# Heads of width 16: operands of 49 rows in two halves of the partitions

## What is computed

```
xr = rope(x)                                   # over the 256 features, before the projection
q, k, v = (xr @ W.T + b for (W, b) in (q, k, v))      # 4 x 16 heads x 512 x 16
p = softmax(q @ k.T / 4)                       # 512 x 512 per head
y = layernorm(x + (p @ v) @ Wo.T + bo)
```

## Time and profile before

| | us |
|---|---|
| three timed runs | 1989.82, 1995.94, 1994.33 (median 1994.33) |
| profiled execution, its own time | 2008.87 |
| its span, first to last instruction | 2007.5 |
| PE busy in the span | 1674.5 (83%) |
| DVE, ACT, POOL busy | 1149.6, 1011.2, 983.3 |

### The profile page before, as it was taken

One profiled execution on the slowest core, in us unless ns is written; L12 is line 12 of the kernel. 1 busy time (PEld: TensorE's weight loads), 2 busy tenths in 40 slices (PEclk: granted clock), 3 DMA queues, 4 the chain that ended last, 5 costly groups with the idle time before them and its releaser, 6 DMA issues. The chain is left out here.

```text
span 2007.5 us, 23647 instructions
## 1 busy us (share of the span) xinstructions
PE 1674.5 (83%) x7418; PEld 1222.8 (61%) x7419; DVE 1149.6 (57%) x2237; ACT 1011.2 (50%) x1933; POOL 983.3 (49%) x832
## 2 busy tenths in 40 slices
PE   5698896699972798989996999989999997589992
PEld 2476675587761465656764666656656665566661
DVE  4665655566645676767745665665575573542223
ACT  2154442455521376766774776666676673142222
POOL 1200000344324266676882775675585584058885
PEclk9899998799996599999998999999999998679996
DMA  2300100544424332222102110121020120248777
GB/s 82 128 12 0 32 22 21 186 109 114 121 45 124 81 82 65 72 64 74 43 21 87 28 44 22 33 62 25 25 67 25 25 60 22 62 98 193 183 181 172
DMA packets 96785, 146.15 MB, mean 73 GB/s; under 512 B 22711, under 2 KB 61820, under 8 KB 93830
## 3 DMA queue, kind: packets, MB, share of 16 engines
q1 hardware_dynamic: 66448, 104.92, 18.1%
q0 software_dynamic: 18432, 26.36, 7.5%
q10 hardware_dynamic: 11782, 13.37, 2.2%
HBM read 101.83 MB, written 36.41 MB: 69 GB/s over the span
## 5 line engine op out<-in xcount | busy, mean ns | idle before, releaser
L2261 POOL TENSOR_TENSOR STp_lo_use<-ST_use,STp_hi_use 128x512 fp32r<-128x512 f32 x256 | 337.7, 1328 | 202.2 <-ACT ST_use L2091 200.9
L1737 POOL TENSOR_TENSOR STp_lo<-ST,STp_hi 128x512 fp32r<-128x512 f32 x192 | 248.2, 1313 | 106.1 <-ACT ST L1512 104.7
L2156 DVE TENSOR_REDUCE nmax_use<-bank 128x1 f32<-128x512 f32 x256 | 173.4, 679 | 111.7 <-PE bank L1996 107.2
L2087 ACT ACTIVATE STp_hi_use<-bank 128x512 fp32r<-128x512 f32 x256 | 152.9, 597 | 163.1 <-PE bank L2022 159.3
L1630 DVE TENSOR_REDUCE nmax<-bank 128x1 f32<-128x512 f32 x256 | 170.9, 683 | 53.8 <-PE bank L1426 53.1
L1426 PE MATMUL bank<-rows_k,rows_q 65*128 65x512 f32 x256 | 135.9, 539 | 38.3 <-DVE nmax L1630 20.5
L2091 ACT ACTIVATE ST_use<-bank 128x512 f32<-128x512 f32 x256 | 151.8, 593 | 2.0 <-POOL STp_lo_use L2261 2.0
L1509 ACT ACTIVATE STp_hi<-bank 128x512 fp32r<-128x512 f32 x192 | 117.0, 609 | 58.0 <-PE bank L1437 57.6
L924 POOL TENSOR_SCALAR veps<-mv 128x4 f32<-128x4 f32 x4 | 0.9, 228 | 253.1 <-DVE mv L873 253.1
L1996 PE MATMUL bank<-ks,qs 128*128 128x512 f32 x256 | 110.5, 432 | 10.2 <-DMA ks<-ks 9.6
L1512 ACT ACTIVATE ST<-bank 128x512 f32<-128x512 f32 x192 | 118.2, 616 | 0.0
(11 more groups left out here) (443 smaller groups left out, 4644.5 us busy)
## 6 DMA issues: line engine op xcount, KB each, us to landing
stage<-in_W SPq DMA_DIRECT2D x16, 1024.0 KB, 4.9
Wgu<-in_Wgu SPq DMA_DIRECT2D x32, 384.0 KB, 3.4
rows_q<-hop_scratch SPq DMA_DIRECT2D x32, 256.0 KB, 4.3
ks<-ks SPq DMA_DIRECT2D x64, 128.0 KB, 2.3
rinv<-rinv_scratch SPq DMA_DIRECT2D x64, 128.0 KB, 2.9
rows_k<-hop_scratch SPq DMA_DIRECT2D x24, 256.0 KB, 5.3
hop_scratch<-qkp_hi SPq DMA_DIRECT2D x20, 256.0 KB
Wda<-in_Wdn SPq DMA_DIRECT2D x32, 128.0 KB, 3.8
```

Of the source, the lines that this page charges most:

```text
L1737: G.tensor_tensor(parts_of(u)[1], ST[u % TB], plain(parts_of(u)[0]), ALU.subtract).then_inc(low.sem, low.inc(u))
L2087: A.activation(STp[u % NHI][0], bk.ap, ACT.Exp)
L2156: V.tensor_reduce(nmax[:, (h % 2) * TB + j:(h % 2) * TB + j + 1], bk.ap, AX.X, ALU.max, negate=True).then_inc(bk.free, 1)
L2261: G.tensor_tensor(STp[u % NHI][1], ST[u % NFULL], plain(STp[u % NHI][0]), ALU.subtract).then_inc(low["pool"].sem, low["pool"].inc(u))
```

## The change

Three blocks of 16 rows take the place of four: q high, q low, q high against k high, k high, k low. The product of the two low parts is left out, and so is the row of zeros, so that the maxima are products over 48 rows and the scores over 49. The two tiles have 128 partitions and half as many slots: heads 0, 1 of each quarter lie in partitions 0 to 48, heads 2, 3 in partitions 64 to 112. `ST_LAG` grows by one step to 24, so the scores are six heads behind the maxima, and the two products of one step use different halves. The projections of the next batch move one step later. A hop of k is two copies as for q; a quarter's operands come in four DMAs each for q and k (128 or 64 KB), and the row of maxima in two. POOL sets all of `rows_k` to one at the start of the stage, in place of the two memsets. The tiles are allocated in another order.

```diff
-    PARTS, MAX_ROW, ROWS = 4 * HD, 4 * HD + 1, 4 * HD + 2
+    PARTS, MAX_ROW, ROWS, HALF = 3 * HD, 3 * HD, 3 * HD + 1, P // 2
-    ST_LAG = SPAN + 7
+    ST_LAG = SPAN + 8
...
-        rows_q, rows_k = sb("rows_q", [ROWS, H1, S], f32r), sb("rows_k", [ROWS, H1, S], f32r)
+        rows_q, rows_k = sb("rows_q", [P, H1 // 2, S], f32r), sb("rows_k", [P, H1 // 2, S], f32r)
...
-        HOPS = {0: ((0, 0), (1, 1)), 1: ((0, 0), (1, 1), (0, 2))}
+        HOPS = ((0, 0), (1, 1))
...
+        def rows_of(rows, h, count):
+
+            first = h // HG % 2 * HALF
+            return rows[first:first + count, h // HS * HG + h % HG, :]
...
-        STACK = ((28, (0, 0), (0, 0)), (31, (1, 0), (0, 1)), (34, (0, 1), (1, 0)), (37, (1, 1), (1, 1)))
+        STACK = ((29, (0, 0), (0, 0)), (32, (1, 0), (0, 1)), (35, (0, 1), (1, 0)), (38, (1, 1), (1, 1)))
...
-                    PE.matmul(bk.ap, rows_q[0:MAX_ROW, h, j * P:(j + 1) * P], rows_k[0:MAX_ROW, h, :], start=True, stop=True).then_inc(bk.full, 1)
+                    PE.matmul(bk.ap, rows_of(rows_q, h, PARTS)[:, j * P:(j + 1) * P], rows_of(rows_k, h, PARTS), start=True, stop=True).then_inc(bk.full, 1)
...
-                    PE.matmul(bk.ap, rows_k[:, h, kt * P:(kt + 1) * P], rows_q[:, h, :], start=True, stop=True).then_inc(bk.full, 1)
+                    PE.matmul(bk.ap, rows_of(rows_k, h, ROWS)[:, kt * P:(kt + 1) * P], rows_of(rows_q, h, ROWS), start=True, stop=True).then_inc(bk.full, 1)
...
+                        A.wait_ge(zeroed.sem, zeroed["rows"])
                         stack_rows(A, 0, i, 1)
...
-            hs = slice(i * HS, (i + 1) * HS)
-            for k in range(2):
-                first = k * n * HD
-                engine.dma_start(plain((rows_q, rows_k)[n][2 * k * HD:2 * (k + 1) * HD, hs]), hop_d[b % 2, n, hs, first:first + 2 * HD].rearrange("h f s -> f h s")).then_inc(stacked[i].sem, stacked[i].step)
+            for p in range(2):
+                hs, at = slice(i * HS + p * HG, i * HS + (p + 1) * HG), slice(i * HG, (i + 1) * HG)
+                for first, count in ((0, 2), (2, 1)) if n == 0 else ((0, 1), (1, 2)):
+                    to = p * HALF + first * HD
+                    engine.dma_start(plain((rows_q, rows_k)[n][to:to + count * HD, at]), hop_d[b % 2, n, hs, 0:count * HD].rearrange("h f s -> f h s")).then_inc(stacked[i].sem, stacked[i].step)
...
         def pool():
+            G.memset(plain(rows_k), 1.0).then_inc(zeroed.sem, zeroed.inc("rows"))
+            G.wait_ge(zeroed.sem, zeroed["rows"])
...
-                    G.memset(plain(rows_q[PARTS:ROWS]), 0.0).then_inc(g_own.sem, g_own.inc("s4 rows_q"))
-                    G.memset(plain(rows_k[PARTS:ROWS]), 1.0).then_inc(zeroed.sem, zeroed.inc("rows"))
-                    G.wait_ge(zeroed.sem, zeroed["rows"])
...
-                        SP.dma_start(plain(rows_q[MAX_ROW:MAX_ROW + 1, i * HS:(i + 1) * HS, :]).rearrange("p h (j q) -> p (h j) q", q=P), plain(rowbuf[i % 2])).then_inc(rowed[i % 2].sem, rowed[i % 2].inc((b, i)))
+                        for p in range(2):
+                            row = p * HALF + MAX_ROW
+                            SP.dma_start(plain(rows_q[row:row + 1, i * HG:(i + 1) * HG, :]).rearrange("p h (j q) -> p (h j) q", q=P), plain(rowbuf[i % 2][p * HG * TB:(p + 1) * HG * TB])).then_inc(rowed[i % 2].sem, rowed[i % 2].inc((b, i, p)))
```

More of the change, by code:

```diff
@@ L1257, in pair @@
             return kit.pair(name, shape, ph)
-        rows_q, rows_k = sb("rows_q", [ROWS, H1, S], f32r), sb("rows_k", [ROWS, H1, S], f32r)
+        rows_q, rows_k = sb("rows_q", [P, H1 // 2, S], f32r), sb("rows_k", [P, H1 // 2, S], f32r)
+        names = ("Wq1", "Wk1", "Wv1")
+        scale = {"Wq1": HD ** -0.5}
+        W = {n: pair(n, [P, DC, D]) for n in names}
+        cs, xT, part, srcp = sb("cs", [P, 2, S]), sb("xT", [P, DC, S]), sb("part", [P, DC, S]), pair("srcp", [P, DC, S])
         Vone = sb("Vone", [P, TB, H1, P], f32r)
@@ L1267, in self_heads @@
         rowbuf = [sb("rowbuf%d" % z, [SPAN, P], f32r) for z in range(2)]
-        names = ("Wq1", "Wk1", "Wv1")
-        scale = {"Wq1": HD ** -0.5}
-        W = {n: pair(n, [P, DC, D]) for n in names}
         bo, bv = sb("bo", [P, D]), sb("bv", [P, D])
         bqkv, bq = sb("bqkv", [P, 3, DC]), sb("bq", [P, DC])
-        cs, xT, part = sb("cs", [P, 2, S]), sb("xT", [P, DC, S]), sb("part", [P, DC, S])
         attT = turned
         stage = [turned[:, :, 0:D], part[:, :, 0:D]]
-        srcp, qkp = pair("srcp", [P, DC, S]), pair("qkp", [P, DC, S])
+        qkp = pair("qkp", [P, DC, S])
         Vc = sb("Vc", [P, TB, D])
@@ L1293, in self_heads @@
         low = Signal(kit, "s4_low", [u for u in range(END) if not whole[u]])
-        rowed = [Signal(kit, "rowed%d" % z, [(b, i) for b in range(B) for i in range(z, QUARTERS, 2)], step=16) for z in range(2)]
+        rowed = [Signal(kit, "rowed%d" % z, [(b, i, p) for b in range(B) for i in range(z, QUARTERS, 2) for p in range(2)], step=16) for z in range(2)]
         weighed = Signal(kit, "s4_weighed")
@@ L1300, in self_heads @@
         stack_high = Signal(kit, "stack_high", [(b, n, g) for b in range(B) for n, g in (((0, 0), (1, 0), (0, 1), (1, 1)) if b == 0 else ((0, 0), (0, 1), (1, 0), (1, 1)))])
-        HOPS = {0: ((0, 0), (1, 1)), 1: ((0, 0), (1, 1), (0, 2))}
-        hopped = [[Signal(kit, "hopped%d_%d" % (n, g), [(b, k) for b in range(B) for k in range(len(HOPS[n]))], step=16) for g in range(DC)] for n in range(2)]
-        stacked = [Signal(kit, "stacked%d" % i, [(b, n) for b in range(B) for n in range(4)], step=16) for i in range(QUARTERS)]
+        HOPS = ((0, 0), (1, 1))
+        hopped = [[Signal(kit, "hopped%d_%d" % (n, g), [(b, k) for b in range(B) for k in range(len(HOPS))], step=16) for g in range(DC)] for n in range(2)]
+        stacked = [Signal(kit, "stacked%d" % i, [(b, n) for b in range(B) for n in range(8)], step=16) for i in range(QUARTERS)]
         placed = Signal(kit, "placed", [(b, g) for b in range(B) for g in range(GROUPS)])
@@ L1422, in pe @@
                     if j == 0 and h % HS == 0:
-                        PE.wait_ge(stacked[h // HS].sem, stacked[h // HS][b, 3])
+                        PE.wait_ge(stacked[h // HS].sem, stacked[h // HS][b, 7])
                     if n:
                         PE.wait_ge(bk.free, n)
-                    PE.matmul(bk.ap, rows_q[0:MAX_ROW, h, j * P:(j + 1) * P], rows_k[0:MAX_ROW, h, :], start=True, stop=True).then_inc(bk.full, 1)
+                    PE.matmul(bk.ap, rows_of(rows_q, h, PARTS)[:, j * P:(j + 1) * P], rows_of(rows_k, h, PARTS), start=True, stop=True).then_inc(bk.full, 1)
                 u = s - ST_LAG
@@ L1433, in pe @@
                         i = h // HS
-                        PE.wait_ge(rowed[i % 2].sem, rowed[i % 2][b, i])
+                        PE.wait_ge(rowed[i % 2].sem, rowed[i % 2][b, i, 1])
                     if n:
                         PE.wait_ge(bk.free, n)
-                    PE.matmul(bk.ap, rows_k[:, h, kt * P:(kt + 1) * P], rows_q[:, h, :], start=True, stop=True).then_inc(bk.full, 1)
+                    PE.matmul(bk.ap, rows_of(rows_k, h, ROWS)[:, kt * P:(kt + 1) * P], rows_of(rows_q, h, ROWS), start=True, stop=True).then_inc(bk.full, 1)
                 u = s - OUT_LAG
@@ L1521, in act @@
                     if b == 0 and g < 2:
-                        A.wait_ge(hopped[1][g].sem, hopped[1][g][0, 2])
+                        A.wait_ge(hopped[1][g].sem, hopped[1][g][0, 1])
                     A.activation(gathered_o[g % 2], bk.ap, ACT.Copy).then_inc(bk.free, 1)
@@ L1528, in act @@
                         if b or i > 1:
-                            A.wait_ge(rowed[i % 2].sem, rowed[i % 2][(b, i - 2) if i > 1 else (b - 1, i + 2)])
+                            A.wait_ge(rowed[i % 2].sem, rowed[i % 2][(b, i - 2, 1) if i > 1 else (b - 1, i + 2, 1)])
                         A.activation(rowbuf[i % 2], ROW_BANK.ap[0:SPAN, 0:P], ACT.Copy).then_inc(ROW_BANK.free, 1)
@@ L1551, in act @@
                         if b:
-                            A.wait_ge(hopped[1 - n][g].sem, hopped[1 - n][g][b if n else b - 1, len(HOPS[1 - n]) - 1])
+                            A.wait_ge(hopped[1 - n][g].sem, hopped[1 - n][g][b if n else b - 1, len(HOPS) - 1])
                         A.activation(stack_out(b, n, 0, g), bk.ap, ACT.Identity, bias=(bqkv[:, 1, g:g + 1] if n else bq[:, g:g + 1]), scale=1.0).then_inc(stack_high.sem, stack_high.inc((b, n, g)))
@@ L1559, in act @@
                     if of_next(s, 43 + i) == 0:
-                        A.wait_ge(hopped[1][i // 2].sem, hopped[1][i // 2][0, 2])
+                        A.wait_ge(hopped[1][i // 2].sem, hopped[1][i // 2][0, 1])
+                        A.wait_ge(zeroed.sem, zeroed["rows"])
                         stack_rows(A, 0, i, 1)
@@ L1597, in hop @@
         def hop(engine, b, n, g):
-            for k, (p, block) in enumerate(HOPS[n]):
+            for k, (p, block) in enumerate(HOPS):
```

(12 more changed lines are left out.)

## The result

The changed kernel takes 2034.62 us in the median (2023.75 to 2046.61, four runs) against 1995.13 for the kernel before (1989.82 to 2004.59, four runs): 1.0194 times as long, with a 95% interval of 1.0124 to 1.0264. That is 39 us more; forecast were 57 and 2051 us. The intervals here and in the table of experiments use only executions within 1.5% of their kernel's fastest, which leaves out one of four (2154.01 us) for the kernel with maxima over 64 rows and three of four for the one with all heads in one half.

The account below looks back on a forecast made before the run. TensorE's stream was taken to bound the stage. Dearer steps +53, tail +6 and data -2 us made +57 us on 1994.33, so 2051 us; the 8-in-10 range was 2022 to 2092.

Parts of the forecast that it names:

- What bounds the stage: Stage's steady heads: TensorE's stream sets the pace at 4.12 us a head, POOL next at 3.94.
- Rival 3: Steady steps: changing height costs nothing and products overlap, so POOL binds; 17 us faster, 1977 us; chance 0.06.
- The price of a change of height: Before the maxima and before the weighted sums of each step: 0.20 us per change in either direction, two a step.
- What the halves give back: Maxima and scores of one step side by side: 0.12 us saved, bounds 0 and 0.23; step grows by 0.25.
- the second product starts 0.11 after the first: Maxima and scores of a step: the scores' weights load over 0.11 us while the maxima stream, saving 0.12 us.
- the lower end given: Growth of a steady step if the whole second product vanishes: 0.40 - 0.23 = 0.17 us.
- How many steps pay: Steps of the four batches: 34, 58, 58 and 62 pay, together 212 x 0.25 = 53 us.
- The tail: Last 24 steps (six heads) of scores and sums after the last maxima, plus one step of lag: +6 us.
- The data: Operand copies at the stage's start: fewer bytes but more DMAs, between -5 and +3 us, taken as -2.
- No overlap: Steady steps: scores wait for the maxima despite the halves, step +0.40 us; +89 us, 2083 us; chance 0.16.
- The clock: Steady steps: a quarter of the 212 falls to half clock, +32 us more, 2083 us; chance 0.11.
- A free change of height: Steady steps: entering and leaving half height costs nothing, steps fall by 0.12 or 0.23 us; 1977 us, chance 0.06.

Follow-up runs that it names:

- the data side alone: Kernel before with three blocks, fewer hops and smaller operand DMAs, still 65 and 66 rows, lag 23: 1994.89 us; repeated, 1998.49 us.

## Why the prediction was right

**What bounds the stage: right.** It was TensorE's stream; a row less in one of its products lengthened the heads by 101 us. The forecast put the room below it at 0.3 us a head until POOL binds, but its own rows give 4.12 - 3.94 = 0.18. Rival 3 would by that gain 10 us and end at 1985, not 1977; since nothing got faster, it did not matter.

**The price of a change of height: right.** 0.20 us from pairs in another stage, of another data type; 0.39 for two was measured in this one, with the late loads that were forecast.

**What the halves give back: too small.** The forecast took 0.12 us and let the scores' weights go in after those of the maxima. The step of the prediction that fails is "the second product starts 0.11 after the first": in the changed kernel 230 of the 232 steps that have both start them within 0.02 us, 3 ns apart in the median, loads and products alike. The saving is 0.23, and a step grew by 0.16 (1.09 - 0.93) instead of 0.25, a little less than the lower end given, 0.17. By the forecast's own terms that end is 1994 + 36 + 6 - 5 = 2031 us, where it wrote 2028; 2034.62 is close above either. The Trainium skill's figure of about 4 ns between row groups (TensorE: Matmul & The Clock Gate, The mechanism), which the forecast set aside for want of a row, agrees with the trace.

**How many steps pay: right in the sum, in part by luck.** From the first to the last maxima the kernel before took 367.1 us (659.2 to 1026.3), the changed one 402.5 (648.6 to 1051.1): +35.4, and 212 x 0.16 to 0.165 is 34 to 35. Batch by batch it holds only for batch 0, which grew by 5.4 us where 34 steps of 0.16 make 5.4. Batches 1 and 2 grew by 12.7 and 11.8 instead of 9.3 each, and batch 3 by 5.5 instead of 9.9. The clock goes the same way: in batches 1 and 2 it was at half speed for 17.1 us each, against 6.8 in the kernel before, and in batch 3 for none, against 3.4. The forecast had no such term, and the errors cancel.

**The tail: right.** From the last maxima to the last scores 23.2 us became 29.9, +6.7 for +6.

**The data: right in kind.** The start took 4.6 us less in the changed kernel and 2.8 and 2.7 less in the kernels with the data side alone, where the forecast had 2. The kernel with all heads in one half has all the copies of the change and gained only 1.5 (54.1), so where the rest of the 4.6 comes from is open. The sign that the forecast named as upsetting, a first maximum before 655 us, did occur (648.6), but 6.0 us of the 10.6 are from before the stage.

The sum with the measured terms is 35.4 + 6.7 - 4.6 = 37.5 us, beside the 39.5 between the medians. The profiled spans are only 14.9 apart, because in this execution of the changed kernel the weights came 6.0 us earlier and the stretch behind the stage was 16.6 us shorter. The second is unchanged code and goes from 943 to 954 us among the other six kernels, with nothing that ties it to the change. If the first belongs to the change, the sum is 31.5, and its agreement with 39.5 is luck.

**The rivals.** No overlap is refuted, by the records and by the kernel with one half. The clock did not decide the changed kernel: it was 1.00 in its steady heads, though batches 1 and 2 spent some 10 us more each at half speed. It did decide the profiled execution of the kernel without overlap. A free change of height is refuted. The Trainium skill's promise of up to 2x for operands of 64 rows or fewer (TensorEngine Tiling (Array Packing), Theoretical Speedup) holds in this trace for the two products taken alone, 0.23 us for both. It is lost on the way in and out.

## What to carry to other kernels

Two products in opposite halves of the array cost as much as one, but entering and leaving the half height costs 0.20 us each time, nearly one 512-column product. One pair gives back 0.23 us and pays 0.40. So such pairs pay only where at least two follow each other between two changes (1.79 us for two steps here, against 1.86), and then the banks and the order of the engines that empty them must allow the burst. In this stream, a single product of 64 rows among taller ones was better padded to 65.

## What the runs showed of the hardware

- One row decides: 65 rows in a stream of 128-row products cost nothing extra, 64 rows cost 0.39 us a step, with the same number of columns. A change between 64 and 65 columns costs nothing.
- Products for the two halves start 3 ns apart in the median, and so do their weight loads.
- At the half clock a change of height costs 0.30 us instead of 0.20 (0.59 for two, in steps of 2.30 us).
- The clock stayed at half for 130 us in which the profile shows PE busy throughout (740 to 870 us), in the kernel with four products in a row and two changes of height a step. Its executions differ by 72 us (2083.39 to 2155.75). The reason is not shown.
